# Two routers interleaved with expert steps, combined weights inside the first norm, and PSUM's eight banks as one store

## The reference, cut to what matters

```python
x = x + 0.5 * L0_ffn(layernorm(x))    # experts of "First"
x = x + L0_attn(layernorm(x))         # 16 heads of 8, biased causal attention
x = x + 0.5 * L0_ffn(layernorm(x))    # the same experts again: "Late"
x = x + 0.5 * L1_ffn(layernorm(x), ...)   # rmsnorm, latent attention with rope, 9 small experts
x = x + L1_attn(layernorm(x), ...)        # gated scan and a small ffn
x = x + 0.5 * L1_ffn(layernorm(x), ...)
```

```python
logits = xf @ Wg                       # the router: 2048 tokens x 8 experts
probs = softmax(logits); top_vals, top_idx = top_k(probs, 2)
loc = running count of each expert's tokens; keep = loc < C
gates = top_vals * keep / max(sum, 1e-9)
hid = einsum('ech,ehf->ecf', inp, W_in); a, g = split(hid, 2)
out_e = einsum('ecf,efh->ech', gelu(a) * g, W_out)
y = (gathered * gates[..., None]).sum(axis=1)
```

## Time and profile before

| what | value |
|---|---|
| median of 3 runs | 1482.75 us (1482.61 to 1486.44) |
| the profiled execution | 1484.72 us |
| its span, first to last instruction | 1483.0 us |
| mean granted TensorE clock | 0.969 of full |
| PE, DVE, ACT, POOL busy | 91%, 68%, 60%, 27% of the span |

### The profile page before, as it was taken

How to read it: one execution, slowest core, us unless ns; L and a number is a source line. 1 busy time by engine, 2 the same in 40 slices (tenths; PEclk the granted TensorE clock), 3 DMA queues, 4 the chain that set the end, 5 groups by cost and what they waited for, 6 DMA issues and landing times.

```text
span 1483.0 us, 27046 instructions
## 1 busy us (share of the span) xinstructions
PE 1345.7 (91%) x10934; PEld 566.0 (38%) x10934; DVE 1001.2 (68%) x1516; ACT 891.3 (60%) x1118; POOL 404.5 (27%) x331
## 2 busy tenths in 40 slices
PE   5899999888876999989998998998889999999997
PEld 3444443333323444433433442443334333434343
DVE  3433677888825447687877768777886597677725
ACT  2334337777783455256566669876588865656672
POOL 5354440100112566452130313015013132102010
PEclk8799999999998999989999999999999999999999
DMA  6622001000003631011110110102001101101100
GB/s 170 115 58 62 21 21 29 17 2 2 2 1 75 144 56 40 1 30 23 34 23 1 23 23 1 23 12 44 1 2 22 23 15 20 30 1 30 23 1 15
DMA packets 30292, 45.80 MB, mean 31 GB/s; under 512 B 5893, under 2 KB 10693, under 8 KB 30117
## 3 DMA queue, kind: packets, MB, share of 16 engines
q1 hardware_dynamic: 30168, 44.08, 13.7%
HBM read 25.39 MB, written 1.18 MB: 18 GB/s over the span
## 4 chain that ended last, share of the span: by engine, by line
PE 76%; ACT 9%; DVE 9%; issue 5%; POOL 1%; ACTq 0%; POOLq 0%; DVEq 0%
PE ps L1179 14%; PE ps L1265 12%; PE ps L1210 7%; PE ps L1145 6%; ACT PR L1338 5%; PE ps L1146 5%; PE ps L1147 5%; PE ps L1165 5%; DVE BM L1415 3%; PE ps L1744 3%; PE ps L1157 2%; PE ps L1229 2%; PE ps L1186 2%; PE ps L1276 2%; PE ps L1225 1%
## 5 line engine op out<-in xcount | busy, mean ns | idle before, releaser
L1338 ACT ACTIVATE PR<-ps 128x1024 f32<-128x1024 f32 x432 | 432.8, 1024 | 209.9 <-PE ps L1186 117.2
L1415 DVE TENSOR_REDUCE BM<-ps 128x2 f32<-128x1024 f32 (+2 forms) x384 | 349.2, 950 | 58.9 <-PE ps L1165 57.6
L1179 PE MATMUL ps<-QS,KS 48*128 48x512 f16 (+7 forms) x2688 | 302.7, 327 | 38.4 <-ACT PR L1338 30.9
L1265 PE MATMUL ps<-PR,VS 128*32 128x512 f32 (+3 forms) x2304 | 234.4, 499 | 3.6 <-ACT PR L1338 3.1
L1165 PE MATMUL ps<-KS,QS 48*128 48x128 f16 (+2 forms) x1728 | 162.6, 274 | 28.7 <-DVE BM L1415 20.3
L1179 PEld LDWEIGHTS ps<-QS,KS 48*128 48x128 f16 (+1 forms) x2688 | 106.7, 95 | 205.8 <-ACT PR L1338 97.1
L1408 DVE TENSOR_REDUCE BM<-ps 128x8 f32<-128x1024 f32 x96 | 116.9, 1220 | 40.8 <-PE ps L1165 40.4
L1165 PEld LDWEIGHTS ps<-KS,QS 48*128 48x128 f16 x1728 | 67.8, 94 | 159.9 <-DVE BM L1415 69.5
L1145 PE MATMUL ps<-YA,QS 128*128 128x512 f16 x256 | 98.6, 385 | 4.6 <-DVE QS L1367 4.5
L1146 PE MATMUL ps<-YA,QS 128*128 128x512 f16 x256 | 98.3, 384 | 0.0
L1147 PE MATMUL ps<-YA,QS 128*128 128x512 f16 x256 | 98.0, 383 | 0.0
(11 more groups left out here) (301 smaller groups left out, 2083.9 us busy)
## 6 DMA issues: line engine op xcount, KB each, us to landing
PR<-gates SPq DMA_DIRECT2D x32, 512.0 KB, 11.4
QS<-KS SPq DMA_DIRECT2D x64, 128.0 KB
QS<-KS SPq DMA_DIRECT2D x64, 64.0 KB
WM<-W_in SPq DMA_DIRECT2D x1, 2048.0 KB, 9.4
QS<-HL SPq DMA_DIRECT2D x48, 32.0 KB
KS<-HL SPq DMA_DIRECT2D x48, 32.0 KB
QS<-CT SPq DMA_DIRECT2D x96, 2.0 KB
KS<-KS SPq DMA_DIRECT2D x8, 128.0 KB, 2.4
```

The lines of the kernel that those rows point to most:

```text
L1179: ins = pe.matmul(ps[pair][:, w, off:off + cols], KS[rows, ks, kt * P:(kt + 1) * P], QS[rows, qs, (ph + 1) * TT - cols:(ph + 1) * TT], sta ...
L1265: ins = pe.matmul(dst[32 * j:32 * j + 32, TT - cols:TT], v, PR[:, buf, j, off:off + cols], start=(g == 0), stop=(g == NGRP[ph] - 1))
L1338: act.activation(dst, src, ACT.Exp, scale=0.125 if lat else 1.0).then_inc(sig["exp"], 1)
L1415: ins = dve.tensor_reduce(BM[:, ph, p, :, qt - 4 * ph, part], bnk[:, :, off:off + nk * P], AX.X, ALU.max)
```

## The change

Six edits, made together.

1. **Routers inside the plans.** `pe_router`, `act_router` and `dve_router` are gone. Their steps are tasks of both plans: `rlg` (16 logit matmuls), 23 tasks `ro`, `rxp` (Exp), `rrk` (both rank matmuls, now into one bank), `rtp` (transpose), `gd` (the DMA that writes the gates). `ro` comes first in DVE's ORDER, and `rlg`, `rrk`, `rtp` have PE priority 0. PE no longer waits for gT before the first `eu`; `exh`, which waits for XN, and `egb`, which needs `gd`, now carry the dependences.
2. **Combined weights inside the first norm.** Their four DMAs stand right behind x's. PE does heads 0 to 3 ahead of the means, heads 4 to 11 between means and variances, and heads 12 to 15 and all of `wo1` behind the variances, into banks 4 and 5. The copies are ACT tasks `cmc` of First, and the variances move to banks 0 to 3.
3. **x's transposes** wait for the identity alone (first count of `s_const`) and no longer for all constants.
4. **Eight banks as one store.** Pairs 0 to 3 may take `sc` and `un`, pairs 0 to 2 the other pair tasks. Singles may stand in any of banks 4 to 7; one whose partner bank is taken is preferred.
5. **Late's weight parts early.** `ewh`/`ewl` 8 to 15 are tasks of First with priority 99 (last), allowed once the last scores of head group 3 are done, into QS slots 0 to 7. Late has no such tasks. Late's heads now use QS slots 8 to 15, and the scan's tiles slots 0 to 7. The DMA group `wl1` needs `egb` 1,3 in the plan.
6. **Rings.** First's ring tiles come in the order RX, HL, OS, ON. `pe_late` waits for `cmc` and for the last Ln (`vln`) of norm 2.

```diff
-    ROOM = {"pair": 3, "misc": 2, "nr": 2}
+    SINGLES = (4, 5, 6, 7)
-             "DVE": ("exl", "ewl", "eup", "eh", "ct", ...
+             "DVE": ("ro", "exl", "ewl", "eup", "eh", "ct", ...
+    def rooms(self, kind, task):
+        if kind == "nr":
+            return [(kind, i) for i in range(2) if (kind, i) not in self.held]
+        busy = {x for r in self.held for x in self.banks(r)}
+        if kind == "pair":
+            return [(kind, i) for i in range(4 if task in ("sc", "un") else 3) if 2 * i not in busy and 2 * i + 1 not in busy]
+        free = sorted((i for i in self.SINGLES if i not in busy), key=lambda i: (i ^ 1 not in busy, -i))
+        return [(kind, i) for i in free[:1]]
...
+        if kind in ("ewh", "ewl") and task[1] >= E:
+            return 99
...
+        if kind in ("rlg", "rrk", "rtp"):
+            return 0
...
+    def router(self):
+        add = self.add
+        x = lg = add("PE", "rlg", ("rlg",))
+        for j in range(STEPS):
+            x = add("DVE", "ro", ("ro", j), x, {12: ("rrk",), 16: ("rxp",), 22: ("rtp",)}.get(j))
+            if j == 1:
+                self.take(lg, "misc", x)
+                add("ACT", "ro", ("rxp",), x)
+            if j == 11:
+                self.take(add("PE", "ro", ("rrk",), x), "misc", ("ro", 13))
+            if j == 21:
+                self.take(add("PE", "ro", ("rtp",), x), "misc", ("ro", 22))
+        add("SP", "egb", ("gd",), x)
...
+    def weights(self):
+        add = self.add
+        for c in range(2 * E):
+            need = ("eu", 2 * c - 4) if 2 <= c < E else ("sc", NQ - 1) + LAST_SC if c >= E else None
+            add("DVE", "ewl", ("ewl", c), add("ACT", "ewh", ("ewh", c), need))
...
         def pe_load(pe):
-            pe.wait_ge(s_const, N_CONST)
+            pe.wait_ge(s_const, 1)
...
         def pe_norm(pe):
+            pe_comp(pe, range(0, 4))
+            pe.wait_ge(s_const, N_CONST)
             pe.wait_ge(s_xup, NT)
             for t in range(NT):
                 pe.matmul(bank(t), mean_w[:, :], XT[:, tsl(t)], start=True, stop=True).then_inc(s_mean, 1)
+            pe_comp(pe, range(4, 12))
             for t in range(NT):
                 pe.wait_ge(s_sq, t + 1)
-                pe.matmul(bank(4 + t), mean_w[:, :], NSQ[:, t, :], start=True, stop=True).then_inc(s_var, 1)
+                pe.matmul(bank(t), mean_w[:, :], NSQ[:, t, :], start=True, stop=True).then_inc(s_var, 1)
+            pe_comp(pe, range(12, H))
+            pe_comp_out(pe)
...
         def slot_of(lat, n):
-            return 4 * (n % 2) if lat else 2 * n
+            return 8 + 4 * (n % 2) if lat else 2 * n
...
         def pe_late(pe):
             plan, c = plan_of(True), counter(True)
-            pe.wait_ge(s_rdv, 6)
-            pe.wait_ge(s_hg, 2)
+            pe.wait_ge(sig["cmc"], 2)
+            pe.wait_ge(sig["vln"], counter(False)("vln", 2, NT - 1))
```

More of the change, by code:

```diff
@@ L221, in cost, with banks @@
         return self.COST[kind]
+    @staticmethod
+    def banks(room):
+        kind, i = room
+        return [2 * i, 2 * i + 1] if kind == "pair" else [i] if kind == "misc" else []
+    def rooms(self, kind, task):
[6 more added lines that the diff above has]
+        return [(kind, i) for i in free[:1]]
     def lead(self):
@@ L313, in simulate @@
                     if task in self.room:
-                        kind = self.room[task]
-                        room = [(kind, i) for i in range(self.ROOM[kind]) if (kind, i) not in self.held]
+                        room = self.rooms(self.room[task], task[0])
                         if not room:
@@ L356, in build @@
     def build(self):
+        self.router()
+        for i in range(2):
+            self.add("ACT", "cm", ("cmc", i))
+        self.frees[("cm",)] = [("cmc", 0), ("cmc", 1)]
+        self.at_first = {("pair", 2): ("cm",)}
         self.experts()
+        self.weights()
         for b in range(B):
@@ L392 @@
     NHE = 11
[L393 removed]
+    table = "exp"
     COST = dict(Plan.COST, **{
@@ L412 @@
              "POOL": ("et", "psg", "pct", "pbt", "on", "xl", "ff", "rot", "xql"),
-             "SP": ("egb", "crow", "put", "kput", "st", "wl1", "wl2")}
+             "SP": ("gd", "egb", "crow", "put", "kput", "st", "wl1", "wl2")}
     def build(self):
+        self.router()
         self.experts()
-        self.add("SP", "wl", ("wl1",), ("ewl", E - 1))
+        self.add("SP", "wl", ("wl1",), ("egb", 1, 3))
         self.add("SP", "wl", ("wl2",), ("ed", 63))
@@ L607, in priority @@
         if eng == "PE":
-            if kind in ("un", "sc", "pv", "turn", "proj", "eu", "ed"):
+            if kind in ("un", "sc", "pv", "turn", "proj", "eu", "ed", "rlg", "rrk", "rtp"):
                 return super().priority(eng, task, t)
@@ L898, in dve_load, with pe_comp, pe_comp_out @@
                 dve.tensor_copy(XT[:, t * TT:(t + 1) * TT], bank(t)).then_inc(s_xup, 1)
+        def pe_comp(pe, heads):
+            pe.wait_ge(s_wc, 64)
+            for h in heads:
+                ins = pe.matmul(bank(4)[:, h * 32:(h + 1) * 32], wqn[:, h, :], wkb[:, h, :], start=True, stop=True)
+            if h == H - 1:
+                ins.then_inc(s_comp, 1)
+        def pe_comp_out(pe):
+            for h in range(H):
+                g, j = divmod(h, QUAD)
+                ins = pe.matmul(bank(5)[32 * j:32 * j + 32, g * P:(g + 1) * P], wkb[:, h, :], won[h // 8][:, h % 8, :],
+                                start=True, stop=True)
+            ins.then_inc(s_comp, 1)
         def pe_norm(pe):
+            pe_comp(pe, range(0, 4))
+            pe.wait_ge(s_const, N_CONST)
             pe.wait_ge(s_xup, NT)
@@ L1015, in dve_router @@
-            dve.wait_ge(s_rpe, 3 * r + 3)
-            dve.tensor_copy(gT[:, :], bank(3)[:, 0:P]).then_inc(s_hg, 1)
+            m = [rt[:, 9, 16 * q:16 * q + 16] for q in range(8)]
+            first = desc[:, :].unsqueeze(1).to_broadcast([P, NTT, E])
+            oh, kept = rt[:, 4, :], rt[:, 8, :]
+            if j in (0, 1):
+                lg = o[:, 0:P].rearrange("p (i e) -> p i e", e=E)
+                if j == 0:
+                    return dve.tensor_reduce(m[0], lg, AX.X, ALU.max)
+                return dve.tensor_tensor(v3(0), lg, over_e(m[0]), ALU.subtract)
@@ L1078, in pe_room_free @@
                 pe.wait_ge(sig["eup"], c("eup", args[0] // 16))
+            elif kind == "rlg":
+                pe.wait_ge(sig["ro"], c("ro", 1))
+            elif kind == "rrk":
+                pe.wait_ge(sig["ro"], c("ro", 13))
+            elif kind == "rtp":
+                pe.wait_ge(sig["ro"], c("ro", 22))
+            elif kind == "cm":
+                pe.wait_ge(sig["cmc"], 2)
             elif kind == "qk":
@@ L1193, in pe_attn @@
             slot = plan.slot.get(task)
-            if kind == "eu":
+            if kind == "rlg":
+                for i in range(NTT):
+                    if i % 4 == 0:
+                        pe.wait_ge(s_xn, normed(lat, i // 4))
+                    ins = pe.matmul(single(plan, task)[:, i * E:(i + 1) * E], XN[:, i * P:(i + 1) * P], w_rt0[:, :],
+                                    start=True, stop=True)
+                ins.then_inc(sig["rlg"], 1)
+            elif kind == "rrk":
+                pe.wait_ge(sig["ro"], c("ro", 11))
+                pe.matmul(single(plan, task)[:, 0:256], lessall[:, :], ohb[:, :], start=True, stop=True)
+                pe.matmul(single(plan, task)[:, 256:512], onesb[:, :], ohb[:, :], start=True, stop=True).then_inc(sig["rrk"], 1)
+            elif kind == "rtp":
+                pe.wait_ge(sig["ro"], c("ro", 21))
+                pe.transpose(single(plan, task)[:, 0:P], rt[:, 0, 0:P], identf[:, :]).then_inc(sig["rtp"], 1)
+            elif kind == "eu":
                 u, = args
@@ L1357, in dve_attn @@
             kind, args = task[0], task[1:]
-            if kind == "exl":
+            if kind == "ro":
+                j, = args
+                src = {0: "rlg", 1: "rlg", 12: "rrk", 13: "rrk", 22: "rtp"}.get(j)
+                if j in (0, 12, 22):
+                    dve.wait_ge(sig[src], c(src))
+                if j == 16:
+                    dve.wait_ge(sig["rxp"], c("rxp"))
+                if j:
+                    dve.wait_ge(sig["ro"], c("ro", j - 1))
+                gate_step(dve, j, single(plan, (src,)) if src else None).then_inc(sig["ro"], 1)
+            elif kind == "exl":
                 t, = args
```

251 lines of the change are left out of this document (115 added, 136 removed).

## The result

The changed kernel takes 1458.51 us (median of 4 runs, 1456.12 to 1461.18), the kernel before, beside it, 1482.68: a ratio of 0.983 with a 95% interval of 0.981 to 0.986. The prediction was 1459.6 and faster. The profiled execution took 1457.45 us, its span 1455.6; by spans the gain is 27.4 us, 3.2 more than by the medians; the experiments show that this difference lies in the opening.

The account below looks back on a forecast made before the run. PE was taken to bound the expert stages, with empty windows at the opening and the turn. Gains 15.9 + 6.2 - 1.0 + 2.0 = 23.1 took the profiled 1484.7 to 1461.6, 1459.6 us for the median; range 1444 to 1474.

Parts of the forecast that it names:

- Opening: Before First's experts: eus start earlier and run ahead of the first et; gain 15.9 us, bounds 12.5 to 18.4.
- Turn: From First's attention to Late's experts: PE runs eus while the router's chain makes the gates; gain 6.2 us.
- Edit 5: First's attention: added ewh and ewl delay scores, a loss of 1.0 us; undone, the turn's gain is gone.
- Edit 4: PE's bank waits, 51 us: the shared store returns a twenty-fifth, a gain of 2.0 us, bounds -6 and +12.
- DVE starves the gates: Both routers: eh goes ahead of ro, gates come 5.5 us later, PE meets a full ring; 1468 us, chance 0.14.
- The clock stays up: Opening: all matmuls behind 18 us run at 2.4 GHz, logits take 3.6 us; 1457 us, chance 0.12.
- The shared store pays: PE's bank waits: the fourth pair returns a third, 17 us and not 2; 1444 us, chance 0.13.
- Slower: Attention's head groups: scores and bounds take the singles' banks, so a turn or first pv waits; 1498 us, chance 0.07.
- no effect: Whole kernel: the junctions' gain is lost again in attention; 1482 us, chance 0.03.

Follow-up runs that it names:

- the repeat: The changed kernel timed and profiled once more, with no edit: 1458.29 us, ratio 0.985 to the kernel before.
- the old rooms: The changed kernel with the PSUM rooms of before, three pairs in banks 0 to 5 and two singles in 6 and 7: 1472.37 us, ratio 0.993.
- run 8: Not a follow-up run: the words come from "PE had run 8 eus", eight expert steps done by the opening's first et.
- The thick run: The changed kernel with three unused f32 matmuls of 512 columns among each router's 16 logit matmuls: 1466.88 us, ratio 0.990.
- the kept order: The changed kernel with Late's order planned as if its weight parts were made in Late, though they are made in First: 1446.53 us, ratio 0.975.
- the kept order with filled waits: The changed kernel, Late's order planned with weight parts in Late, plus 8 unused f32 matmuls ahead of two long PE waits: 1443.23 us, ratio 0.973.
- eu at 1.29: The kernel before, replanned with the planner's cost of eu at 1.29 and not 1.28, same instructions in another order: 1505.75 us, ratio 1.014.
- logits at 4.2: The changed kernel, replanned with the planner's cost of the logits at 4.2 and not 4.6, same program in another order: 1444.10 us, ratio 0.973.

## Why the prediction was right, and where not

**Opening (predicted 15.9, bounds 12.5 to 18.4; measured 16.6, or 13 to 15 for openings of one kind).** The end of the step is right, its parts are not all. XN was expected at 27.6 and was complete at 25.01: the norm's matmuls ran at 2.4 GHz and the weights' passes between them took 1.97 and 1.07 us, so PE's earlier start was not spent again. In the repeat, with means at the lower clock, it was complete at 28.65; the forecast stands between the two. The logits take 5.99 us, between the two bounds, because the clock falls inside them; the eus start cold as in the earlier trace rows. The gates' DMA was issued at 41.05 and the broadcast at 42.64, 1.6 us later where the earlier trace rows gave 3.5. Together the first et came at 48.72 (51.86 in the repeat) and not 50.7. Against that PE had run 8 eus by then and not 10.5: a gap of 2.96 us for the transpose was foreseen, but it woke with the clock at half rate again until 44.64, and that was not. Earlier gates and fewer eus cancel, which is luck.

**Turn (6.2, bounds 4.5 to 6.8; measured 8.2, turn and Late's experts together).** The mechanism held: the first et comes 3.3 us later behind First's last Exp than before (37.47 against 34.19; 1.7 were expected), and PE is ahead all the same. The term that was too small is the run ahead. Part of that is a slip in the sum: 3 eus, 1 us, one eu and 3 us take 9.2 of the 17.3, which leaves 8.1 us and not 7.4, so 10.3 eus and a gain of 7.0. The two eh fell into the chain's own wait for the rank matmul, the gap for the transpose was 1.67 us and not 3, and PE had run about 11 eus at the first et. Against that, the eus were expected at the full clock and the first eight passes took 1.6 us more behind the thin logits.

**Edit 5 (cost 1.0; undone, the turn's gain is gone).** Its cost in First's attention is 0.3 us with the store (219.78 against 219.47); with the old rooms that stretch is 2.2 above before (224.67 against 222.48). Undone, the turn's gain falls from 8.2 to 3.1: most of it goes, not all. But not for the reason given. The prediction had the ewl behind the chain and the eus waiting for them; in the run they fit in beside it and the eus start at once, and with the parts made early and the order kept the turn is as long. What the 5 us hang on is how many eh the planner puts into the chain's gap. What the prediction left out is that moving tasks out of Late redraws Late's order. That order cost 12.7 us in Late's attention, so in this kernel edit 5 is a net loss.

**Edit 4 (gain 2.0, bounds -6 and +12; on net 2.3 in Late's attention, 2.7 with edit 5 in First's, -2.5 at the end).** The total agrees, which says little. Undone alone it costs 14 us, above the bound; done alone it gives 5. In First's attention, where redrawing moved the stretch by 0.1 and 1.8 us and two executions of one order differ by up to 2.2, it is worth 3.0 to 4.9. In Late's, the three orders with the old rooms took 812.3, 819.3 and 832.4, the distinct ones with the store 810, 797 and 799: better in each, by an amount between 2 and 35 that depends on which two orders are compared. The planner's own figures have it at 15 to 27. The term took back a twenty-fifth of the 51 us of waits; the traces have 5 to 17 us less of them. So the term was too small in the waits it was built from, and what the changed kernel's order lost elsewhere hid it. The prediction named the order "the real uncertainty" and still gave it a bound of 12; one draw is worth up to 20 us there, nearly as much as all six edits.

**The rivals.** "DVE starves the gates" is real but needs another order of DVE: 12.8 us in all. "The clock stays up" is refuted, the logits ran at 0.59 granted. "The shared store pays" had a third of the bank waits returned, and against the old rooms the traces show just that (58.5 to 41.5 us). That the same program in another order takes 1444.10, beside its 1444, is a coincidence. "Slower" and "no effect": no turn or first pv was held up so that it showed among PE's longest waits. But the point made for "slower", that the planner's costs need not be the chip's, is where the changed kernel lost its 12 us: 8.8 in slower matmuls, the rest in waits.

**Still open.** What in this opening brings the clock down inside gapless logits: the thin weights' matmuls ahead of them or the first thin passes themselves. The thick run does not separate them, and its second router is one execution. Edit 3 was not tried alone: that PE starts with x at 7.59 is read from the trace. That DVE and POOL slow each other was not made an experiment of its own; the redrawn orders move the two together and apart, see below. And the order-kept turn could not be joined with the changed kernel's (180 with 797), which by the stretches would give another 5 us by estimate.

The fastest version was the kept order with filled waits, 1443.23 (0.973, 0.971 to 0.974); the redrawn one at 1444.10 can't be told from it. Both beat the kernel before and the changed one.

## What to carry to other kernels

Where a planner writes the order, compare a change over several orders (move a cost by a hundredth and plan again), or keep the order fixed; a single before and after measures the draw along with the edit. Compare plan and chip stretch by stretch, and where the chip adds more, look for a wait of PE with half the clock behind it: there the wait costs more than its length (5 us and about 4 more in the case above). Thin matmuls can bring the clock down without any wait, so look at what stands ahead of dense work too. And a serial chain of short instructions hides well beside throughput work, if it comes first on the engine that both share and the work can run ahead of its result.

## What the runs showed of the hardware

The same DVE instructions took 2.65 and 3.02 us while POOL's tensor_tensor ran beside them, and 0.82 and 1.27 without; POOL's own 2.24 us for ON stand against 1.27 at the turn's et. The orders separate the two by themselves. With the kernel before, the old rooms or eu at 1.29, DVE and POOL hardly overlap there and the instruction of 3.02 us takes 1.27. With the kept order and with logits at 4.2 two of its kind overlap with POOL throughout and take 2.24, and there is no wait of 5.0 us. The Trainium skill (SBUF — State Buffer, SBUF: two separate sides) says that VectorE and GpSimd share a pair of ports as an exclusive lock; times up to three times as long on DVE and nearly twice on POOL fit that. The reduction out of PSUM took 1.21 us beside POOL, and 1.18 to 1.23 in all its 96 places.

Thin matmuls without a gap lowered the clock: behind 32 logit passes of 8 columns the eu passes were 0.427 us apart in ten of ten traces, and 0.215 in the one with three matmuls of 512 columns among the logits.

Between the two profiled executions of the changed kernel the opening varies by 3.5 us: x lands 0.9 us later and the first norm's means find another clock. In other pairs a later stretch varies by up to 2.2 us.
